# A vision transformer block with mixture of experts on one core: the shared expert moved behind the block loop, one embedding moved into the front of a stage

## The chip, the cores and the metric

The kernel runs on one core of a Trainium2 chip. The metric is the device time of one execution in microseconds. Times within the profile are microseconds from the start of the span. PE is TensorE, DVE is VectorE, ACT is ScalarE, POOL is GpSimd, SP is SyncE, which issues most DMAs.

## The reference

32 images of 36 patches and one class token give 1184 tokens of width 256, all in float32. With `ln` a normalisation without weights:

```
h = concat(cls, patches(x) @ W.T + b + pos)              # 32 x 37 x 256
# attention, per image, 16 heads of 16, no softmax
a = ln(h); q, k = silu(a Wq), silu(a Wk); v = a Wv; q, k = rope(q), rope(k)
o = ((q k^T) * lower_triangle) v * sigmoid(a Wg1 Wg2)
h = h + (ln(o) * ln_w + ln_b) @ Wo
# feed forward
y = ln(h); s = sigmoid(y @ gate.T)
# 6 of 32 experts out of the best 2 of 4 groups by s + bias; weights s / sum * 0.2
routed = sum_e w_e * (silu(y Wg_e) * (y Wu_e)) Wd_e
shared = (silu(y Sg) * (y Su)) Sd                        # hidden 128
anchor = 0.1 * the same form, one of 16 small experts
h = h + routed + shared + anchor
```

## The kernel before

The tokens lie in 11 tiles: ten of 111 tokens (three images) and one of 74. Two tiles make a block; there are six blocks, the last with one tile. `P` is 128, `D` 256, `KC` 2 (halves of the width), `BT` 222 tokens of a block, `NB` 6, `NT` 11. PSUM has eight banks, `B[0]` to `B[7]`.

**The block loop.** Each engine has its own instruction list written out by hand, and semaphores tie them. Stage j of the loop works on up to four blocks at once (`stage`): `coming` = j + 1 is embedded, `ahead` = j gets first norm, q, k, v and rope, `mid` = j - 1 gets energies, attention, gate and `Wo`, `last` = j - 2 gets second norm, routing, choice of experts, ranks in the lists and the shared expert. The order within a stage on PE is that of the loop at L612; on ACT L798, on DVE L1079. Stage 1 is the first with a `mid`, stage 2 the first with a `last`; stage 5 has no `coming`, stage 6 neither `coming` nor `ahead`.

What PE calls there, with its lines: `energies` L509 (32-row products in banks 4 to 7), `second_transposes` L552, `route` L564 (scores in bank 0), `shared_up` L590 (bank 3), `attend` L524 (bank 2), `normed_transposes` L456, `embed` L432 (12 products of 256 columns a tile, bank 0), `out_project` L538 and L541 (bank 3 for the first tile of a block, 7 for the second), `rank` L576 to L581 (bank 1), `project` L466 and L472, `rotate` L487, `gate_inner` L479, `shared_down` L601 (bank 0), `gate` L495. Each float32 product of PE leaves two records in the trace.

On DVE: `mask_energy` L1014 (four masks a tile), `shared_mult` L1051, `apply_gate` L1024, `choose` L912 to L952, `attended` L1035 to L1043, `place` L961 to L968 (gives `slot_ok`), `embedded` L976, `rope` L997 to L1007, `norms` L896 to L899, `shared_add` L1057. On ACT: `second_norm` and `first_norm` L731, `second_copy` L783, `shared_silu` L794, `scores` L789 (Sigmoid), `normed_copy` L743, `squares` L774, `qkv_copies` L749 (Silu) to L757, `split_heads` L768, `gate_tanh` L762.

**Bank 0 and its order.** `embed`, `route` and `shared_down` share bank 0. So `embed` of block b waits for the sigmoids of block b - 3 (`rt_ok`), `route` for `shared_add` of the block before (`hs_ok`) and for `h_emb`, and `shared_down` for `h_emb` too.

**The lists.** When `place` has given a block's slots, GpSimd scatters each tile's rows to the lists in DRAM, seven scatters a tile (L388): first the anchor row of both tiles, then the six expert rows of each. Three scatters of tile 9 stand behind the anchor row of tile 10. So the 14 scatters of a full block and, from block 4 on, the last 21 are in one queue, and behind them on the same engine are the additions of the list stage (L408).

**Behind the loop** the last block is routed and ranked, DVE computes a table of list tiles (L1114 to L1151), PE turns it into a row (`table_rows`, L608 and L610). SP then waits for the anchor scatters and for the table and loads rows (L355). The list stage takes 112 tiles of 128 rows: transposes (L673), up (L685), down (L694), weighing on ACT (L851), addition to `sums_d` on GpSimd (L408). PE begins it behind `hs_ok` = `NB`, the last shared addition. The weights of all experts replace the buffers of the block loop in `W`: `load_late` is issued by SP when `h_emb` and `h2_ok` say that those buffers are free.

The functions are printed with the line numbers of the profile:

Of the kernel before, what the change touches and what calls it, by code (L numbers as in the profile page):

```python
# [24 lines left out]
P = 128  # L25
D = 256
# [50 lines left out]
def build(nc, pt, wt, posr, brow, wqkv, wo, wg1, wg2, lnwb, gwt, gbias, sgu, sd, wx,  # L77
          ident_c, cmask_c, turn_c, parity_c, cs_c, before_c, small_c, out):
    with ExitStack() as ctx:
# [70 lines left out]
        g1T = sb("g1T", [HD, BT])  # L150
        s_gate = sb("s_gate", [P, BT])
        s_hid = sb("s_hid", [P, BT])
        e_sb = sb("e_sb", [P, 2 * HEADS * TT])
# [264 lines left out]
        def _(pe):  # L418
            def embed(b, i):
                t, at = BLOCKS[b][i], i * TT  # L420
                if b:
                    pe.wait_ge(ld[f"patch{b}"], 16)
                if i == 0 and b:
                    pe.wait_ge(h_emb, b)
                    if b == 2:
                        pe.wait_ge(fold_ok, 1)
                    if b >= 3:
                        pe.wait_ge(rt_ok, b - 2)
                for c in range(PC):
                    if b == 0 and i == 0:  # L430
                        pe.wait_ge(chunk[c], 32)
                    m = pe.matmul(B[0][0:TILES[t], i * D:(i + 1) * D], patch_view(b)[:, c, at:at + TILES[t]],  # L432
                                  w_patch[:, c, :], start=c == 0, stop=c == PC - 1)
                if i == len(BLOCKS[b]) - 1:
                    m.then_inc(emb_ps, 1)
# [93 lines left out]
            def out_project(b):  # L529
                pe.wait_ge(og_ok, b + 1)  # L530
                if b == 0:
                    pe.wait_ge(fold_ok, 1)
                else:
                    pe.wait_ge(sh_ok, b)
                for t in BLOCKS[b]:
# [18 lines left out]

            def route(b):
                pe.wait_ge(x2T_ok, b + 1)
                if b:
                    pe.wait_ge(hs_ok, b)
                if b + 2 < NB:
                    pe.wait_ge(h_emb, b + 3)  # L560
                for t in BLOCKS[b]:
                    (i, _), n, r = within(b, t), TILES[t], t * TT
                    for k in range(KC):
                        m = pe.matmul(B[0][0:n, i * EXPERTS:(i + 1) * EXPERTS], x2T[:, k, r:r + n], w_route[:, k, :],  # L564
                                      start=k == 0, stop=k == KC - 1)
                m.then_inc(rt_ps, 1)
# [18 lines left out]
            def shared_up(b):  # L585
                n, r = SIZES[b], FIRST[b]
                pe.wait_ge(h2_ok, BLOCKS[b][-1] + 1)
                for m in range(2):
                    for k in range(KC):
                        mm = pe.matmul(B[3][:, m * BT:m * BT + n], w_sgu[:, k, m * P:(m + 1) * P], x2T[:, k, r:r + n],  # L590
                                       start=k == 0, stop=k == KC - 1)
                mm.then_inc(su_ps, 1)

            def shared_down(b):
                pe.wait_ge(sh_ok, b + 1)
                pe.wait_ge(rt_ok, b + 1)
                if b + 3 < NB:
                    pe.wait_ge(h_emb, b + 4)
                for t in BLOCKS[b]:
                    (i, at), n = within(b, t), TILES[t]  # L600
                    m = pe.matmul(B[0][0:n, i * D:(i + 1) * D], s_hid[:, at:at + n], w_sd[:, :], start=True, stop=True)  # L601
                m.then_inc(sd_ps, 1)
# [9 lines left out]
            for j in range(-1, NB + 1):  # L612
                coming, ahead, mid, last = stage(j)
                tiles = BLOCKS[mid] if mid is not None else []
                if mid is not None:
                    energies(mid, tiles[0])
                if last is not None:
                    second_transposes(last)
                for t in tiles[1:]:
                    energies(mid, t)  # L620
                if last is not None:
                    route(last)
                    shared_up(last)
                if mid is not None:
                    attend(mid, tiles[0])
                if ahead == 0:
                    pe.wait_ge(ld["consts"], 16 * 8)
                if ahead is not None:
                    normed_transposes(ahead)
                for t in tiles[1:]:  # L630
                    attend(mid, t)
                if ahead == 0:
# [3 lines left out]
                    gate(ahead)  # L636
                if coming is not None:
                    embed(coming, 0)
                if mid is not None:
                    out_project(mid)  # L640
                if last is not None:
                    rank(last)
                if coming is not None and len(BLOCKS[coming]) > 1:
                    embed(coming, 1)
                if ahead == 0:
                    pe.wait_ge(ld["rest"], 16 * 8)
                    fold()
                elif ahead is not None:
                    project(ahead)
                    rotate(ahead)  # L650
                    gate_inner(ahead)
                if last is not None:
                    shared_down(last)
                if ahead is not None and ahead > 0:
                    gate(ahead)
            second_transposes(NB - 1)
            route(NB - 1)
            shared_up(NB - 1)
            rank(NB - 1)
            table_rows()  # L660
            shared_down(NB - 1)
# [48 lines left out]
        def _(act):  # L710
# [74 lines left out]
            def scores(b):  # L785
                act.wait_ge(rt_ps, b + 1)
                for t in BLOCKS[b]:
                    i, n = t - BLOCKS[b][0], TILES[t]
                    m = act.activation(sig[0:n, i, :], B[0][0:n, i * EXPERTS:(i + 1) * EXPERTS], ACT.Sigmoid)  # L789
                m.then_inc(rt_ok, 1)  # L790

            def shared_silu(b):
                act.wait_ge(su_ps, b + 1)
                act.activation(s_gate[:, 0:SIZES[b]], B[3][:, 0:SIZES[b]], ACT.Silu).then_inc(ss_ok, 1)  # L794

            act.wait_ge(ini, 1)
            act.activation(warm[:, :], ones[:, 0:1], ACT.Silu)
            for j in range(0, NB + 1):  # L798
# [6 lines left out]
                if last is not None:  # L805
                    shared_silu(last)
                    scores(last)
# [13 lines left out]
            scores(NB - 1)  # L821
            shared_silu(NB - 1)

# [39 lines left out]
        def _(dve):  # L863
# [184 lines left out]
            def shared_mult(b):  # L1048
                n = SIZES[b]
                dve.wait_ge(ss_ok, b + 1)  # L1050
                dve.tensor_tensor(s_hid[:, 0:n], s_gate[:, 0:n], B[3][:, BT:BT + n], ALU.mult).then_inc(sh_ok, 1)  # L1051

            def shared_add(b):
                dve.wait_ge(sd_ps, b + 1)
                t0, k, n = BLOCKS[b][0], len(BLOCKS[b]), TILES[BLOCKS[b][0]]
                rows = h[0:n, t0:t0 + k, :]
                dve.tensor_tensor(rows, B[0][0:n, 0:k * D].rearrange("p (k d) -> p k d", k=k), rows, ALU.add).then_inc(hs_ok, 1)  # L1057

# [20 lines left out]
            for j in range(-1, NB + 1):  # L1079
                coming, ahead, mid, last = stage(j)  # L1080
                for t in BLOCKS[mid] if mid is not None else []:
                    mask_energy(mid, t)
                if last is not None:
                    shared_mult(last)
                if mid is not None:
# [17 lines left out]
                if ahead == 0:  # L1103
                    dve.wait_ge(ld["rest"], 16 * 8)
                    fold()
                    add_bias(ahead)
                if last is not None:
                    shared_add(last)
            choose(NB - 1)
# [12 lines left out]
            step(dve.tensor_tensor(starts, ends, tiles_of, ALU.subtract))  # L1122
            shared_mult(NB - 1)

# [21 lines left out]
            dve.tensor_scalar(weight_c, weight_c, float(D), None, ALU.add).then_inc(cols_ok, 1)  # L1146

            dve.wait_ge(table_ps, 1)
            dve.tensor_copy(table[:, :, :].rearrange("p a b -> p (a b)"), B[6][0:1, 0:3 * P])

            dve.tensor_scalar(fresh[:, :], B[6][:, 3 * P:4 * P], pcol, None, ALU.is_le).then_inc(table_ok, 1)  # L1151
            dve.wait_ge(table_ok, 1)
            shared_add(NB - 1)

# [117 lines left out]
```

## Time and profile before

| | |
|---|---|
| median of 3 runs | 495.29 us (494.2 to 495.57) |
| profiled execution | 495.58 us, span 493.8 us |
| block loop | 38 to 219 us |
| end of the loop, table, first list rows | 219 to 247 us |
| list stage | 246 to 471 us |
| last sums and output | 471 to 494 us |

Read it in that order: each part has a different limit, and the engines' shares over the whole span say little. The granted clock is given as a share of full speed: 1.00 is 2.4 GHz, 0.50 is 1.2 GHz, and a value between is a mean over a stretch with both.

### The profile page before, as it was taken

The numbers are of one execution on the slowest core, as the hardware profiler recorded it, in microseconds if no ns is written. First come the engines' busy times: TensorE is split into PE (matmuls) and PEld (weight loads), VectorE is DVE, ScalarE is ACT, GpSimd is POOL, SyncE is SP. The second block draws the span as 40 slices with busy tenths as digits, with TensorE's granted clock in tenths as the row PEclk, the third lists the DMA queues.
The fourth block names the chain that finished last, engine by engine and source line by source line (L and its number), as shares of the span: only waits on it lengthen the run. The fifth ranks groups of instructions, "written<-read, shape, count | busy, mean of one in ns | idle before, by whom it ended". The sixth has DMA issues, their size and how long they took to land.

```text
span 493.8 us, 10106 instructions
## 1 busy us (share of the span) xinstructions
PE 370.2 (75%) x2456; PEld 302.3 (61%) x2457; DVE 261.3 (53%) x1088; ACT 203.1 (41%) x581; POOL 291.4 (59%) x205
## 2 busy tenths in 40 slices
PE   6488989989899786641277879999998898998000
PEld 4465858768677565531156557778887787787000
DVE  0336585957948848378145554444444444444045
ACT  1131143232332332210035556767776767767100
POOL 3000000383682863878587888888888888888533
PEclk9797978969879668655669999999999999999655
DMA  8999996032133861378458999999999999997795
GB/s 242 306 336 306 439 365 212 18 78 63 39 86 82 344 140 20 82 236 293 103 140 153 161 155 155 157 151 155 158 152 155 157 150 155 158 153 120 143 255 177
DMA packets 66303, 85.81 MB, mean 174 GB/s; under 512 B 16840, under 2 KB 61302, under 8 KB 65894
## 3 DMA queue, kind: packets, MB, share of 16 engines
q1 hardware_dynamic: 35734, 59.82, 39.1%
q0 software_dynamic: 29680, 24.95, 34.9%
q10 hardware_dynamic: 864, 0.73, 0.5%
q8 instruction: 12, 0.20, 0.2%
q14 instruction: 13, 0.11, 0.1%
HBM read 45.86 MB, written 39.47 MB: 173 GB/s over the span
## 4 chain that ended last, share of the span: by engine, by line
DVE 20%; PE 19%; issue 19%; DMA 17%; ACT 10%; POOL 8%; ACTq 4%; SPq 1%; DVEq 0%; POOLq 0%
DMA sums_d<-e_sb,tok 13%; POOL rows_d L388 5%; ACT UPW L831 4%; PE B L524 3%; PE B L590 3%; ACTq L274 3%; PE B L509 3%; PE B L432 2%; POOL sums_d L408 2%; ACT e_sb L851 2%; DMA W<-in_brow 2%; DMA W<-sums_d 2%; PE B L564 2%; PE B L466 2%; DVE h L1186 1%
## 5 line engine op out<-in xcount | busy, mean ns | idle before, releaser
L408 POOL DMA_INDIRECT sums_d<-e_sb,tok x112 | 174.0, 1554 | 35.3 <-issue 23.5
L388 POOL DMA_INDIRECT rows_d<-xrow,slot x77 | 105.2, 1366 | 146.0 <-issue 114.7
L685 PEld LDWEIGHTS B<-e_sb,UPW 128*128 128x128 f32 x796 | 105.7, 193 | 10.7 <-issue 5.2
L685 PE MATMUL B<-e_sb,UPW 128*128 128x128 f32 x796 | 109.7, 279 | 0.0
L694 PE MATMUL B<-W,e_sb 128*128 x224 | 73.5, 410 | 20.3 <-DVE e_sb L1177 10.3
L1177 DVE TENSOR_TENSOR e_sb<-e_sb,B 128x128 f32<-128x128 f32 (+1 forms) x112 | 32.2, 288 | 81.1 <-ACT e_sb L839 61.1
L831 ACT COPY UPW<-W 128x512 f32 (+1 forms) x112 | 63.0, 563 | 17.9 <-issue 17.7
L673 PE MATMUL B<-ident,e_sb 128*128 128x128 f32 x224 | 44.8, 283 | 14.1 <-DMA e_sb<-rows_d 13.1
L694 PEld LDWEIGHTS B<-W,e_sb 128*128 128x128 f32 x224 | 34.0, 191 | 33.5 <-issue 33.0
L851 ACT ACTIVATE e_sb<-B,wcol 128x256 f32<-128x256 f32 x112 | 53.0, 473 | 0.2 <-issue 0.2
L1161 DVE COPY e_sb<-B 128x256 f32<-128x256 f32 x112 | 46.9, 419 | 11.2 <-PE B L673 10.4
L850 ACT COPY tok<-tok_of 128x1 int32 (+1 forms) x112 | 21.5, 192 | 58.4 <-DMA sums_d<-e_sb,tok 44.8
L673 PEld LDWEIGHTS B<-ident,e_sb 128*128 128x128 f32 x224 | 28.0, 145 | 17.6 <-issue 10.7
L839 ACT ACTIVATE e_sb<-B 128x128 f32<-128x128 f32 (+1 forms) x112 | 30.7, 275 | 19.6 <-PE B L685 11.9
L432 PE MATMUL B<-W 128*111 128x256 f32 (+1 forms) x132 | 34.3, 414 | 4.7 <-DMA W<-in_pt 4.7
L432 PEld LDWEIGHTS B<-W 128*111 128x111 f32 (+1 forms) x132 | 24.0, 189 | 12.1 <-DMA W<-in_pt 5.1
L1163 DVE TENSOR_TENSOR wcol<-e_sb,fresh (+1 forms) x112 | 17.8, 159 | 24.9 <-issue 21.7
L509 PE MATMUL B<-W 32*111 32x222 f32 (+1 forms) x176 | 21.3, 521 | 11.5 <-ACT W L768 9.1
L1014 DVE TENSOR_TENSOR e_sb<-B,causal 111x444 f32<-111x444 f32 (+1 forms) x44 | 23.5, 596 | 6.4 <-PE B L509 6.3
L749 ACT ACTIVATE W<-B 128x444 f32<-128x444 f32 (+1 forms) x12 | 6.0, 500 | 44.3 <-PE B L466 44.3
L509 PEld LDWEIGHTS B<-W 32*111 32x111 f32 (+1 forms) x176 | 13.6, 239 | 16.3 <-ACT W L768 10.6
L1186 DVE TENSOR_TENSOR h<-h,W 112x256 f32<-112x256 f32 (+3 forms) x15 | 12.7, 867 | 19.0 <-DMA W<-sums_d 11.4
(165 smaller groups left out, 470.7 us busy)
## 6 DMA issues: line engine op xcount, KB each, us to landing
e_sb<-rows_d SPq DMA_DIRECT2D x112, 152.5 KB
rows_d<-padrow SPq DMA_DIRECT2D x1, 7320.0 KB, 34.5
W<-in_wx SPq DMA_DIRECT2D x1, 7027.0 KB, 50.4
sums_d<-padrow SPq DMA_DIRECT2D x4, 1408.0 KB, 22.4
W<-in_wx SPq DMA_DIRECT2D x1, 4781.0 KB, 17.2
W<-in_wx SPq DMA_DIRECT2D x1, 4576.0 KB
W<-in_pt SPq DMA_DIRECT2D x4, 666.0 KB, 8.8
sums_d<-e_sb,tok POOLq DMA_INDIRECT x112
```

The lines of the kernel that those rows point to most:

```text
L388: pool.indirect_dma_start(rows_d, bass.IndirectOffsetOnAxis(ap=slot[0:n, t, j:j + 1], axis=0), xrow[0:n, t, :], None).then_inc(done, 16)
L408: pool.indirect_dma_start(sums_d[c], bass.IndirectOffsetOnAxis(ap=tok[:, c:c + 1], axis=0), Y[:, c, :], None, compute_op=ALU.add).then_inc ...
L432: m = pe.matmul(B[0][0:TILES[t], i * D:(i + 1) * D], patch_view(b)[:, c, at:at + TILES[t]], w_patch[:, c, :], start=c == 0, stop=c == PC - 1)
L509: m = pe.matmul(B[4 + r][0:n, 2 * k * n:2 * (k + 1) * n], qk[strip, KC + k, at:at + n], q_two[strip, :, k, at:at + n], start=True, stop=True)
L673: m = pe.transpose(B[u % 2][:, k * P:(k + 1) * P], G[:, u % 4, k * P:(k + 1) * P], ident[:, :])
L685: mm = pe.matmul(B[2 + u % 2][:, m * P:(m + 1) * P], UPW[:, u % 2, at:at + P], GT[:, u % 2, k, :], start=k == 0, stop=k == KC - 1)
L694: pe.matmul(B[6 + u % 2][:, 0:D], H[:, u % 2, :], W[:, bass.ds(e, size)][:, at:at + D], start=True, stop=True).then_inc(D_ps, 1)
L831: act.copy(UPW[:, u % 2, 0:n], weights[:, 0:n]).then_inc(upw_ok, 1)
L839: act.activation(S[0:n, u % 2, :], B[2 + u % 2][0:n, 0:P], ACT.Silu).then_inc(silu_ok, 1)
L851: act.activation(Y[:, u % 4, :], B[6 + u % 2][:, 0:D], ACT.Copy, scale=wcol[:, bass.ds(i, 1)]).then_inc(Y_ok, 1)
L1161: dve.tensor_copy(GT[:, v % 2, :, :].rearrange("p k s -> p (k s)"), B[v % 2][:, 0:D]).then_inc(gt_ok, 1)
L1177: dve.tensor_tensor(H[0:n, u % 2, :], S[0:n, u % 2, :], ups, ALU.mult).then_inc(H_ok, 1)
```

## The change

`route` writes its scores to bank 3 in place of bank 0, so the waits of `embed`, `route` and `shared_down` on each other fall away, and `out_project` waits for the sigmoids (`rt_ok`). `shared_up`, `shared_silu`, `shared_mult`, `shared_down` and `shared_add` leave the loop on all three engines. They run for all six blocks behind it, `shared_up` in banks 4 and 5 in turn, `shared_down` in banks 0 and 3, with two buffers each of `s_gate` and `s_hid`. On PE block 0's `shared_up` stands ahead of the last `rank`; on DVE two multiplications and one addition stand in and behind the table's computation, the others behind it, ahead of the first list rows.

In a stage, the first tile's embedding moves from ahead of `out_project` to right behind the first tile's energies (in stages 1 to 4; stage 0 keeps it behind the gate). The first attend moves ahead of `route`, `normed_transposes` behind the last attend, and the second tile's embedding ahead of `rank`.

```diff
 # embed
-                    if b >= 3:
-                        pe.wait_ge(rt_ok, b - 2)
 # out_project
-                    pe.wait_ge(sh_ok, b)
+                    pe.wait_ge(rt_ok, b)
 # route: B[0] -> B[3]
-                if b:
-                    pe.wait_ge(hs_ok, b)
-                if b + 2 < NB:
-                    pe.wait_ge(h_emb, b + 3)
+                pe.wait_ge(h2_ok, BLOCKS[b][-1] + 1)
 # shared_up: B[3] -> B[4 + b % 2]
-                pe.wait_ge(h2_ok, BLOCKS[b][-1] + 1)
+                if b < 2:
+                    pe.wait_ge(en_ok, 4 * NT)
+                else:
+                    pe.wait_ge(sh_ok, b - 1)
 # shared_down: B[0] -> B[3 * (b % 2)]
-                pe.wait_ge(rt_ok, b + 1)
-                if b + 3 < NB:
-                    pe.wait_ge(h_emb, b + 4)
+                if b < 2:
+                    pe.wait_ge(rt_ok, NB)
+                else:
+                    pe.wait_ge(hs_ok, b - 1)
 # the stages on PE
                     energies(mid, tiles[0])
+                if coming is not None and ahead != 0:
+                    embed(coming, 0)
                 if last is not None:
                     second_transposes(last)
                 for t in tiles[1:]:
                     energies(mid, t)
+                if mid is not None:
+                    attend(mid, tiles[0])
                 if last is not None:
                     route(last)
-                    shared_up(last)
-                if mid is not None:
-                    attend(mid, tiles[0])
+                for t in tiles[1:]:
+                    attend(mid, t)
                 if ahead == 0:
                     pe.wait_ge(ld["consts"], 16 * 8)
                 if ahead is not None:
                     normed_transposes(ahead)
-                for t in tiles[1:]:
-                    attend(mid, t)
                 if ahead == 0:
                     project(ahead)
                     rotate(ahead)
                     gate_inner(ahead)
                     gate(ahead)
-                if coming is not None:
                     embed(coming, 0)
                 if mid is not None:
                     out_project(mid)
+                if coming is not None and len(BLOCKS[coming]) > 1:
+                    embed(coming, 1)
                 if last is not None:
                     rank(last)
-                if coming is not None and len(BLOCKS[coming]) > 1:
-                    embed(coming, 1)
...
-                if last is not None:
-                    shared_down(last)
-                if ahead is not None and ahead > 0:
                     gate(ahead)
 # PE behind the loop
             route(NB - 1)
-            shared_up(NB - 1)
+            shared_up(0)
             rank(NB - 1)
-            table_rows()
+            for b in range(1, NB):
+                shared_up(b)
+                if b == 2:
+                    table_rows()
+                shared_down(b - 1)
             shared_down(NB - 1)
 # ACT: out of the loop, behind the last scores
-                    shared_silu(last)
-            shared_silu(NB - 1)
+            for b in range(NB):
+                shared_silu(b)
 # DVE: out of the loop, in and behind the table
-                if last is not None:
-                    shared_mult(last)
-                if last is not None:
-                    shared_add(last)
-            shared_mult(NB - 1)
+            shared_mult(0)
...
+            shared_mult(1)
+            shared_add(0)
             dve.wait_ge(table_ps, 1)
...
             dve.wait_ge(table_ok, 1)
+            for b in range(2, NB):
+                shared_mult(b)
+                shared_add(b - 1)
             shared_add(NB - 1)
```

## Rows read from the trace of the kernel before

**Rows 1.** Windows from first energies to gate, stages 2 to 6, one gate to energies
```profile
core 0: us, PE busy (x) PEld busy (x) DVE busy (x) ACT busy (x) POOL busy (x), PEclk, DMA share, GB/s
67.38:80.26 12.88, 11.93 (x121) 9.16 (x122) 5.67 (x15) 5.32 (x11) 0.00 (x0) 0.60 1.07 378
...
99.57:113.54 13.97, 12.64 (x121) 9.85 (x122) 6.28 (x16) 5.43 (x11) 11.24 (x9) 0.63 0.33 76
113.54:132.79 19.25, 18.10 (x95) 14.76 (x95) 17.46 (x80) 5.32 (x12) 8.60 (x6) 1.00 0.20 45
132.79:146.49 13.70, 13.27 (x124) 10.22 (x125) 6.28 (x17) 5.32 (x11) 11.10 (x9) 0.63 0.35 82
...
165.11:179.57 14.46, 12.91 (x118) 9.84 (x118) 6.42 (x16) 4.70 (x10) 11.72 (x10) 0.58 0.90 274
...
194.41:205.51 11.10, 8.19 (x68) 6.45 (x68) 3.84 (x15) 3.55 (x8) 9.20 (x7) 0.54 0.32 68
```

**Rows 2.** Timeline of POOL: start, us, engine, line, operation, [idle before <-releaser]
```profile
192.40 1.48 POOL L388 DMA_INDIRECT rows_d<-xrow,slot  x1 [10.45 <-DVE slot L968]
...
217.50 1.35 POOL L388 DMA_INDIRECT rows_d<-xrow,slot  x1 [2.10 <-DVE slot L968]
...
256.20 1.62 POOL L408 DMA_INDIRECT sums_d<-e_sb,tok  x1 [0.30 <-issue]
```

**Rows 3.** Timeline of ACT, stage 3 and the first result of the lists
```profile
114.79 1.28 ACT L749 ACT_TABLE_LOAD   x1
124.12 0.54 ACT L749 ACTIVATE W<-B 128x444 f32<-128x444 f32 x1 [8.05 <-PE B L466]
...
254.07 0.47 ACT L851 ACTIVATE e_sb<-B,wcol 128x256 f32<-128x256 f32 x1
```

**Rows 4.** Timeline of PE, stage 1
```profile
38.83 1.02 PE L509 MATMUL B<-W 32*111 32x222 f32 x16
42.23 2.95 PE L509 MATMUL B<-W 32*111 32x222 f32 x16 [2.37 <-DVE e_sb L1014]
...
49.32 3.63 PE L432 MATMUL B<-W 128*111 128x256 f32 x12
...
55.24 2.83 PE L432 MATMUL B<-W 128*111 128x256 f32 x12
```

**Rows 5.** Timeline of DVE, stages 1 and 3
```profile
40.18 0.77 DVE L1063 SCALAR_TENSOR_TENSOR W<-B,W 128x256 f32<-128x256 f32 x2
...
44.49 2.20 DVE L1014 TENSOR_TENSOR e_sb<-B,causal 111x444 f32<-111x444 f32 x4 [0.84 <-PE B L509]
...
129.22 1.14 DVE L1005 TENSOR_TENSOR W<-B,cossin 128x444 f32<-128x444 f32 x2
```

**Rows 6.** Timeline of PE, stage 3
```profile
101.91 0.84 PE L552 MATMUL B<-ident,xrow 111*128 111x111 f32 x4 [1.33 <-ACT xrow L731]
102.68 2.62 PE L509 MATMUL B<-W 32*111 32x222 f32 x16
105.24 1.70 PE L564 MATMUL B<-w_route,x2T 128*111 128x32 f32 x8
...
112.50 0.98 PE L524 MATMUL B<-e_sb,W 111*32 111x111 f32 x32
113.41 2.85 PE L432 MATMUL B<-W 128*111 128x256 f32 x12
...
129.60 1.12 PE L601 MATMUL B<-w_sd,s_hid 128*111 128x256 f32 x4
```

**Rows 7.** Timeline of PE: `shared_up` in stage 3
```profile
106.75 3.31 PE L590 MATMUL B<-x2T,w_sgu 128*128 128x222 f32 x8
```

**Rows 8.** Window of stage 3 at the lower clock (columns as in rows 1)
```profile
102.40:112.40 10.00, 10.00 (x70) 7.84 (x69) 3.62 (x7) 3.44 (x7) 8.17 (x7) 0.50 0.35 82
```

**Rows 9.** Timeline of PE: first energies of stage 5, last `shared_up`, first list rows
```profile
165.11 1.83 PE L509 MATMUL B<-W 32*111 32x222 f32 x16 [3.05 <-ACT W L768]
...
221.26 1.97 PE L590 MATMUL B<-x2T,w_sgu 128*128 128x74 f32 x8
...
246.79 0.66 PE L673 MATMUL B<-ident,e_sb 128*128 128x128 f32 x2 [8.31 <-DMA e_sb<-rows_d]
```

More of the change, by code:

```diff
@@ L150, in build @@
         g1T = sb("g1T", [HD, BT])
-        s_gate = sb("s_gate", [P, BT])
-        s_hid = sb("s_hid", [P, BT])
+        s_gate = sb("s_gate", [P, 2, BT])
+        s_hid = sb("s_hid", [P, 2, BT])
         e_sb = sb("e_sb", [P, 2 * HEADS * TT])
@@ L563, in route @@
                     for k in range(KC):
-                        m = pe.matmul(B[0][0:n, i * EXPERTS:(i + 1) * EXPERTS], x2T[:, k, r:r + n], w_route[:, k, :],
+                        m = pe.matmul(B[3][0:n, i * EXPERTS:(i + 1) * EXPERTS], x2T[:, k, r:r + n], w_route[:, k, :],
                                       start=k == 0, stop=k == KC - 1)
@@ L585, in shared_up @@
             def shared_up(b):
-                n, r = SIZES[b], FIRST[b]
-                pe.wait_ge(h2_ok, BLOCKS[b][-1] + 1)
+                n, r, bank = SIZES[b], FIRST[b], B[4 + b % 2]
+                if b < 2:
+                    pe.wait_ge(en_ok, 4 * NT)
+                else:
+                    pe.wait_ge(sh_ok, b - 1)
                 for m in range(2):
                     for k in range(KC):
-                        mm = pe.matmul(B[3][:, m * BT:m * BT + n], w_sgu[:, k, m * P:(m + 1) * P], x2T[:, k, r:r + n],
+                        mm = pe.matmul(bank[:, m * BT:m * BT + n], w_sgu[:, k, m * P:(m + 1) * P], x2T[:, k, r:r + n],
                                        start=k == 0, stop=k == KC - 1)
@@ L595, in shared_down @@
                 pe.wait_ge(sh_ok, b + 1)
-                pe.wait_ge(rt_ok, b + 1)
-                if b + 3 < NB:
-                    pe.wait_ge(h_emb, b + 4)
+                if b < 2:
+                    pe.wait_ge(rt_ok, NB)
+                else:
+                    pe.wait_ge(hs_ok, b - 1)
                 for t in BLOCKS[b]:
                     (i, at), n = within(b, t), TILES[t]
-                    m = pe.matmul(B[0][0:n, i * D:(i + 1) * D], s_hid[:, at:at + n], w_sd[:, :], start=True, stop=True)
+                    m = pe.matmul(B[3 * (b % 2)][0:n, i * D:(i + 1) * D], s_hid[:, b % 2, at:at + n], w_sd[:, :],
+                                  start=True, stop=True)
                 m.then_inc(sd_ps, 1)
@@ L788, in scores @@
                     i, n = t - BLOCKS[b][0], TILES[t]
-                    m = act.activation(sig[0:n, i, :], B[0][0:n, i * EXPERTS:(i + 1) * EXPERTS], ACT.Sigmoid)
+                    m = act.activation(sig[0:n, i, :], B[3][0:n, i * EXPERTS:(i + 1) * EXPERTS], ACT.Sigmoid)
                 m.then_inc(rt_ok, 1)
@@ L793, in shared_silu @@
                 act.wait_ge(su_ps, b + 1)
-                act.activation(s_gate[:, 0:SIZES[b]], B[3][:, 0:SIZES[b]], ACT.Silu).then_inc(ss_ok, 1)
+                if b >= 2:
+                    act.wait_ge(sh_ok, b - 1)
+                act.activation(s_gate[:, b % 2, 0:SIZES[b]], B[4 + b % 2][:, 0:SIZES[b]], ACT.Silu).then_inc(ss_ok, 1)
             act.wait_ge(ini, 1)
@@ L1050, in shared_mult @@
                 dve.wait_ge(ss_ok, b + 1)
-                dve.tensor_tensor(s_hid[:, 0:n], s_gate[:, 0:n], B[3][:, BT:BT + n], ALU.mult).then_inc(sh_ok, 1)
+                if b >= 2:
+                    dve.wait_ge(sd_ps, b - 1)
+                dve.tensor_tensor(s_hid[:, b % 2, 0:n], s_gate[:, b % 2, 0:n], B[4 + b % 2][:, BT:BT + n],
+                                  ALU.mult).then_inc(sh_ok, 1)
             def shared_add(b):
@@ L1056, in shared_add @@
                 rows = h[0:n, t0:t0 + k, :]
-                dve.tensor_tensor(rows, B[0][0:n, 0:k * D].rearrange("p (k d) -> p k d", k=k), rows, ALU.add).then_inc(hs_ok, 1)
+                dve.tensor_tensor(rows, B[3 * (b % 2)][0:n, 0:k * D].rearrange("p (k d) -> p k d", k=k), rows, ALU.add).then_inc(hs_ok, 1)
             def fold():
```

## The prediction

> **What bounds the kernel now.** I began with the page's slices, where TensorE's granted clock falls again and again in the block loop and stays high in the list stage. The profiled execution took 495.58 us, its span 493.8; the median of the runs is 495.29, so the sum below is made against 495.58 and brought down by 0.3 at its end.
>
> Then the windows of the block loop [rows 1], cut at two events of each stage: the first energies on PE and `apply_gate` on DVE. From the first energies to the gate (the front) a stage takes 12.88, 13.97, 13.70, 14.46 and 11.10 us; from the gate to the next first energies (the back) 19.25 in a full stage. In the back DVE is busy 17.5 us of 19.3: choice, norms, placing and rope in one chain. In the front DVE is busy about 6 us and waits for PE. So in a front PE's order sets the time, in a back DVE's. The clock is 0.54 to 0.63 of full in a front and 1.00 in a back: the chip grants 1.2 GHz over most of the front.
>
> Next GpSimd [rows 2]. A scatter takes 1.35 us and 0.30 before the next: 1.65. The 14 of one block begin at 192.40; the first of the next block at 217.50, after an idle time of 2.10. From there 21 scatters run (21 × 1.65 = 34.7; a gap of 4 us is in the rest), and the first addition of the list stage follows directly at 256.20. The first result of the list stage is ready at 254.07 + 0.47 = 254.54 [rows 3], so GpSimd binds here, by 1.7 us. The change touches nothing of the 112 list tiles. What the change gives is therefore how much earlier the scatters of blocks 8, 9 and 10 end.
>
> **Stage 1 (38 to 67).** Between the first tile's energies, over at 39.85, and the second tile's, which begin at 42.23 because the masks are late, PE has nothing [rows 4]. After the change the first tile's embedding stands there. It waits for `fold_ok`, given at 40.95 [rows 5], so it runs from 41.0 to 43.8 (2.85 us, the embedding at the full clock [rows 6]). The second energies follow to about 45, DVE's four masks, 2.20 us as before [rows 5] and begun with the first of these energies, end at 46.7, and the last attend takes 0.98 [rows 6]: gate at 47.7 against 49.46. The old front is followed by a 3.63 us embedding and `out_project` to 55.24 [rows 4]; now `out_project` (2.3) has ahead of it only the wait for the gate, some 0.7 us, and in it that for the squares, 0.6. The second tile's embedding would begin near 51.5 instead of 55.24. Gain 3.7 us, 2.5 if the clock falls here as it did before.
>
> **Fronts of stages 2, 3, 4.** Removed: `shared_up`, 3.31 us [rows 7], and `normed_transposes` (four small products, about 0.6) moves behind the last attend. Added: embedding of one tile, between the first energies and the second transposes. A wait of 1.33 us for the second norm, which stood there [rows 6], is covered. The price of the embedding depends on the clock: 2.85 at the full clock, at the half clock up to nearly twice that, 5.4; no row shows it wholly at half (3.63 is mixed [rows 4]). In stage 3 the clock was at 0.50 from 102.4 to 112.4 [rows 8], after a pause on PE, and 1.00 before and behind. The pause before the first energies now gets longer, because PE loses 4.0 us of work in the back (2.85 embedding, 1.12 `shared_down` [rows 6]) and gains some 1.5 of waiting. So I take it that the clock falls, and that twelve dense 256-column records bring it back before the front ends: 4.3 us, between the ends. The front is then: first energies 1.83 [rows 9], embedding 4.3, transposes 0.9, second energies 1.8 (1.02 [rows 4] to 2.62 [rows 6]), attend 0.98, route 1.0 (1.70 at the half clock; at full between half of that and 1.70), attend 0.98 = 11.8 us. Gains 1.1, 2.2 and 1.9: 5.2 together. Wholly at the full clock the front is 1.02 + 2.85 + 0.6 + 1.02 + 0.98 + 1.70 + 0.98 = 9.1: gains 3.8, 4.9, 4.6 = 13.3. Wholly at half it is 1.83 + 5.4 + 1.0 + 2.62 + 1.7 + 1.7 + 1.7 = 15.9: a loss of 3.0, 1.9 and 2.2 = 7.1.
>
> **The backs stay.** PE after the gate: wait for gate and squares, `out_project` to +3.6, embedding of the second tile +6.3, `rank` +7.6 (its `ch_ok` comes at +5), `project` 3.1, values 1.8, `rotate` 1.6: +14.1. DVE needs the rotated halves at +15.7 (129.22 against the gate at 113.54 [rows 1, 5]), so there are 1.6 us of cover; it was 0.4 before. If the clock is still half through `out_project` and this embedding (+1.5 and +2.7), the cover is gone and rope is late by some 2.6 us in that stage. `shared_mult` (0.4) and `shared_add` (0.68) leave DVE: the first stood in its wait, the second delays masks that nobody waits for; nothing. Removing the `rt_ok` wait and moving the scores to Wo's bank make `out_project` wait for the sigmoids; these follow `route` by 0.4 us while the last attend takes 0.98, so nothing.
>
> The sigmoid needs its own table in each stage, and the Silu of q and k the other; these two loads of 1.28 us stay. ScalarE does the load ahead of the wait for the operand [rows 3]: its load is at 114.79, the Silu at 124.12 after 8.05 us of waiting. So both lie in its idle time. Were the sigmoid's load behind `route` all the same, load and sigmoids would take 1.28 + 0.3 = 1.6, against 0.98 + 0.62 for attend and gate that choice waits for anyway: nothing either way. The Trainium skill ("ScalarE: Activation LUTs", What ACT_TABLE_LOAD costs) gives 2.66 us for a switch with its drain and would have the calls batched by set. By its figure, with the load behind `route`, choice would come 1.4 us late in each of stages 2 to 5, and the sum would be 5.4 us less; the trace has the load ahead of the wait.
>
> **Stage 5 (165 to 194)** has no embedding to take in. Front: 1.83, wait 0.55, transposes 1.0, energies 2.6, attend 1.7, route 1.7, attend 1.7 = 11.1, and of the old front's 14.46 us PE is busy 12.91 [rows 1], so that beside the wait of 0.55 another 1.0 is idle that I can't explain and leave in for a third: 11.4 against 14.46, gain 3.1 (2.4 to 3.4).
>
> **Stage 6 (194 to 217).** `shared_up` (3.3) is gone, the table load no longer follows a late Silu (1.28): choice starts 7.1 us after the first energies, not 11.4 (the front of 11.10 and the gate's 0.3): 4.3 earlier. But GpSimd has the block before to scatter, from 192.40 to 215.40, and it started again at 217.50 [rows 2]. Of its 2.10 idle us it can lose all but the usual 0.30: it gains 1.8 only.
>
> **The shared tail.** All of it moves behind the loop: five blocks of 3.3 up and 2.0 down at the half clock plus the small one. It must be done before PE takes the first list rows (246.79 [rows 9]; those wait for a load that waits for the anchor scatters), and 1.7 us of slack follow. In times of the old trace and at the half clock: up(0) 221.3 [rows 9] to 224.8, `rank` to 226.3, up(1) to 229.6, down(0) to 231.8, up(2) to 235.1, table rows at 235.8 as now. Then down(1), up(3), down(2), up(4), down(3), up(5), down(4), down(5): 3 × 2.0 + 2 × 3.3 + 2.0 + 2.0 + 1.0, some 17 at half, 9 at the full clock, from 238 or 239: `hs_ok` at 248 to 256. All of this comes 4.3 − 1.8 = 2.5 earlier against GpSimd: 245.5 to 253.5 against 246.8 + 1.7. Dense work has then gone on from 221, so I take the fast end: nothing. The slow end costs 5.0.
>
> **Sum.** 3.7 + 5.2 + 3.1 + 1.8 = 13.8. 495.58 − 13.8 = 481.8 by the profile, 481.5 as a median.
>
> **The rivals.**
> *Clock stays up* (0.15): the dense embedding prevents the fall. For it: in stage 1 PE pauses 1.2 us, not 2.4. Against: the pause will be about 3 us, as the one before 165.11 [rows 9], and that front had 0.58 in the mean [rows 1]. 13.3 instead of 5.2: 473.4.
> *Clock stays down through the fronts* (0.14): −7.1 instead of 5.2, stage 1 at 2.5: 495.0; halfway, 489. For it: ten microseconds at 0.5 in the old front of stage 3 [rows 8] with energies and dense products mixed.
> *The tail is exposed* (0.12): half clock through it: 481.5 + 5.0 = 486.5.
> *TensorE becomes the chain in stages 2 to 4* (0.04, the slower one): half clock reaches into the back; the front loses 2.4 in the mean and rope is 2.6 late, 5.0 a stage. Stages 1, 5, 6 give 8.6, so it decides from 3.4 us lost a stage on (1.5 us over no change); at 5.0 it is 495.3 − 8.6 + 15.0 = 501.7.
> *The change does nothing* (0.03): the list stage's start hangs on something that doesn't move, weights in W say; but `load_late` is itself released by `h_emb` and `h2_ok`, which move: 495.
>
> The main case has the rest, 0.52, with 478 to 485 of its own. What a measurement here can't tell from no change is 0.3%, 1.5 us. Faster takes main, warm, tail and four fifths of the cold one; same the do-nothing case and a part of the cold one: 0.91, 0.05, 0.04. The range reaches from the warm case to the middle of the cold one: 473.5 to 490.
>
> **What would show it.** The first scatter after 210 some 14 us earlier (near 204) and 14 scatters before it without a gap; fronts of 11 to 12 us in stages 2 to 4, stage 5 near 11.4; `out_project` in stage 1 ending near 51.5; embeddings after the first energies at 3.6 to 5.0 us; backs still 19.3; the last `shared_add` before or just at the first landing of list rows. Wrong it would be if the embedding takes over 5 us and the clock is 0.5 up to the gate, if DVE waits for `rotate` in a back, or if PE's first list transposes follow the last shared product at once, later than 8 us ahead of GpSimd's first addition.

## The result and the profile after

The changed kernel takes 478.28 us (median of 4 runs) against 494.75 before: a ratio of 0.9673, interval 0.9632 to 0.9713, so 16.5 us less. Its span is 476.3 us against 493.8. Forecast were 481.5, with 473.5 to 490 as the range. Each ratio in this text is to the kernel before as it ran on the same occasion, with a 95% interval; its medians there lie between 494.2 and 497.0 us, so versions of different occasions are compared by their ratios.

The windows of the block loop in the changed kernel, cut as in [rows 1]: first energies to gate (front), gate to first energies (back), stages 2 to 6. Line numbers of the changed kernel are 2 lower on PE in the loop and 6 higher on DVE.

```profile
core 0: us, PE busy (x) PEld busy (x) DVE busy (x) ACT busy (x) POOL busy (x), PEclk, DMA share, GB/s
...
64.17:72.62 8.45, 7.98 (x121) 6.28 (x122) 5.27 (x14) 4.56 (x9) 0.00 (x0) 1.00 1.02 365
72.62:91.93 19.31, 14.99 (x82) 12.28 (x82) 17.52 (x80) 5.74 (x13) 5.14 (x4) 0.95 0.51 171
91.93:102.72 10.79, 10.31 (x121) 7.73 (x122) 5.40 (x15) 4.55 (x9) 8.66 (x8) 0.77 0.32 71
...
121.97:133.06 11.09, 10.62 (x121) 7.31 (x122) 5.45 (x15) 4.55 (x9) 8.96 (x8) 0.75 0.34 81
133.06:151.92 18.86, 15.66 (x70) 13.00 (x70) 16.94 (x78) 5.74 (x13) 10.43 (x8) 0.82 0.51 168
151.92:160.40 8.48, 7.20 (x110) 5.63 (x110) 5.28 (x15) 4.06 (x8) 6.76 (x6) 0.80 0.88 321
160.40:176.22 15.82, 13.26 (x65) 11.63 (x64) 13.41 (x72) 4.09 (x10) 9.43 (x7) 0.65 0.45 100
176.22:181.17 4.95, 3.56 (x55) 2.63 (x55) 2.80 (x13) 2.55 (x5) 4.03 (x4) 0.50 0.30 74
```

The fronts of stages 2 to 5 went from 12.88, 13.97, 13.70 and 14.46 us to 8.45, 10.79, 11.09 and 8.48, and their granted clock from about 0.6 to 0.75 and more. The backs of stages 2 and 3 stayed at 19.3.

PE in the front of stage 3 (timeline, as [rows 6]). The pause of 3.69 us before it is new (it was 1.20); the first energies and most of the embedding run at the half clock, and all behind them at the full one.

```profile
91.93 1.84 PE L507 MATMUL B<-W 32*111 32x222 f32 x16 [3.69 <-ACT W L772]
93.70 4.37 PE L430 MATMUL B<-W 128*111 128x256 f32 x12
97.90 0.54 PE L550 MATMUL B<-ident,xrow 111*128 111x111 f32 x4
98.38 1.02 PE L507 MATMUL B<-W 32*111 32x222 f32 x16
99.33 0.97 PE L522 MATMUL B<-e_sb,W 111*32 111x111 f32 x32
100.23 0.96 PE L560 MATMUL B<-w_route,x2T 128*111 128x32 f32 x8
101.67 0.98 PE L522 MATMUL B<-e_sb,W 111*32 111x111 f32 x32 [0.47 <-DVE e_sb L1020]
```

GpSimd (timeline, as [rows 2]): the 14 scatters from 173.22 run into the next block's at 196.76 with no wait for slots; then one stop of 5.52 us, and the first additions.

```profile
173.22 1.48 POOL L388 DMA_INDIRECT rows_d<-xrow,slot  x1 [4.76 <-DVE slot L974]
...
196.76 1.35 POOL L388 DMA_INDIRECT rows_d<-xrow,slot  x1 [0.30 <-issue]
...
225.11 1.35 POOL L388 DMA_INDIRECT rows_d<-xrow,slot  x1 [5.52 <-issue]
...
236.68 1.62 POOL L408 DMA_INDIRECT sums_d<-e_sb,tok  x1 [0.30 <-issue]
240.75 1.59 POOL L408 DMA_INDIRECT sums_d<-e_sb,tok  x1 [2.44 <-ACT e_sb L857]
```

In the kernel before the same stop was shorter, and the second addition did not wait:

```profile
244.63 1.35 POOL L388 DMA_INDIRECT rows_d<-xrow,slot  x1 [4.28 <-issue]
...
258.12 1.59 POOL L408 DMA_INDIRECT sums_d<-e_sb,tok  x1 [0.30 <-issue]
```

So the time can be followed: at the first energies of stage 6 the gain is 194.41 − 176.22 = 18.2 us; at block 4's first scatter 217.50 − 196.76 = 20.7; at the first addition 256.20 − 236.68 = 19.5, since the stop grew by 1.2; at the end of the span 17.5. The last 2.0 went at the very start of the list stage: GpSimd waits 2.44, 0.52 and 1.04 us ahead of its second, third and fourth addition, where it waited 0.30, 0.30 and 1.46 before, and from the fourth addition (263.03 against 245.45) to the 109th the gain stays at 17.6. The chain of work now runs through transfers there (start, us, what): the last anchor row lands 9.36 us after its scatter is issued, and the load of the rows for the second result takes 5.22 us.

```profile
214.94 9.36 DMA rows_d<-xrow,slot
...
224.97 2.28 DMA e_sb<-rows_d
...
231.74 5.22 DMA e_sb<-rows_d
```

The tail: the last shared products end at about 222, and PE then waits 5.27 us for list rows.

```profile
220.62 1.49 PE L603 MATMUL B<-w_sd,s_hid 128*111 128x256 f32 x6
227.38 0.66 PE L677 MATMUL B<-ident,e_sb 128*128 128x128 f32 x2 [5.27 <-DMA e_sb<-rows_d]
```

### The profile page after: what moved, and what is told of

It is laid out like the page before. It is cut to its first block, busy times and chain, and to the rows that moved or that the text cites. A ratio compares the mean times of both kernels' runs of the same rounds, so it can differ in the third digit from the quotient of the medians.

```text
span 476.3 us, 10113 instructions
## 1 busy us (share of the span) xinstructions
PE 361.7 (76%) x2456; PEld 299.7 (63%) x2457; DVE 261.3 (55%) x1088; ACT 201.6 (42%) x581; POOL 291.6 (61%) x205
## 4 chain that ended last, share of the span: by engine, by line
DMA 29%; PE 18%; DVE 17%; issue 13%; POOL 13%; ACT 6%; ACTq 2%; SPq 1%; POOLq 0%; DVEq 0%
DMA sums_d<-e_sb,tok 22%; POOL rows_d L388 7%; POOL sums_d L408 5%; PE B L430 5%; PE B L464 3%; ACT e_sb L857 2%; PE B L507 2%; DMA rows_d<-xrow,slot 2%; DMA W<-sums_d 2%; DMA W<-in_brow 2%; DMA e_sb<-rows_d 2%; DVE e_sb L1020 2%; DVE h L1196 2%; ACTq L274 2%; PE B L522 1%
## 5 line engine op out<-in xcount | busy, mean ns | idle before, releaser
L689 PEld LDWEIGHTS B<-e_sb,UPW 128*128 128x128 f32 x796 | 108.1, 197 | 10.8 <-issue 4.5
L689 PE MATMUL B<-e_sb,UPW 128*128 128x128 f32 x796 | 111.4, 282 | 0.0
L698 PE MATMUL B<-W,e_sb 128*128 x224 | 75.1, 418 | 20.1 <-DVE e_sb L1187 18.3
L677 PE MATMUL B<-ident,e_sb 128*128 128x128 f32 x224 | 45.4, 286 | 10.2 <-DMA e_sb<-rows_d 10.0
L430 PE MATMUL B<-W 128*111 128x256 f32 (+1 forms) x132 | 35.9, 430 | 5.7 <-DMA W<-in_pt 4.5
L845 ACT ACTIVATE e_sb<-B 128x128 f32<-128x128 f32 (+1 forms) x112 | 30.8, 275 | 17.4 <-PE B L689 10.8
L464 PE MATMUL B<-W 128*128 128x222 f32 (+1 forms) x96 | 24.5, 426 | 0.6 <-ACT W L747 0.6
L464 PEld LDWEIGHTS B<-W 128*128 128x128 f32 x96 | 22.2, 255 | 1.8 <-ACT W L747 1.0
```

The source lines that it names most:

```text
L464: m = pe.matmul(B[4 + half][:, c * BT:c * BT + n], w_qkv[:, k, lo:lo + P], xnT[:, k, 0:n], start=k == 0, stop=k == KC - 1)
L677: m = pe.transpose(B[u % 2][:, k * P:(k + 1) * P], G[:, u % 4, k * P:(k + 1) * P], ident[:, :])
L689: mm = pe.matmul(B[2 + u % 2][:, m * P:(m + 1) * P], UPW[:, u % 2, at:at + P], GT[:, u % 2, k, :], start=k == 0, stop=k == KC - 1)
L698: pe.matmul(B[6 + u % 2][:, 0:D], H[:, u % 2, :], W[:, bass.ds(e, size)][:, at:at + D], start=True, stop=True).then_inc(D_ps, 1)
```

## The experiments

### The early embedding undone

The first tile's embedding stands ahead of `out_project` again, behind `normed_transposes` (cut short):

```diff
-                if coming is not None and ahead != 0:
-                    embed(coming, 0)              # behind energies(mid, tiles[0])
...
+                if coming is not None and ahead != 0:
+                    embed(coming, 0)              # ahead of out_project(mid)
```

> The changed kernel with one part undone: in stages 1 to 4 the first tile's embedding stands behind normed_transposes and ahead of out_project again. Theory (the early embedding fills PE's pauses and brings the clock up early): stage 1 loses 3.7 us again, the fronts of stages 2 to 4 are no shorter without it (about 11 us at the half clock, against 8.45, 10.79, 11.09), so 478.3 + 3.7 + 2.5 = 484.5 us. Rival (leaving the shared expert out of the front did it all, the embedding only costs there): fronts of about 8 us or less in stages 3 and 4, stage 1 alone loses: 478.3 + 3.7 - 5 = 477 us.

482.51 us, ratio 0.9782 (0.9717 to 0.9847), just clear of the changed kernel's interval. Fronts of stages 2 to 4 (windows):

```profile
66.57:76.65 10.08, 8.86 (x109) 6.94 (x110) 5.26 (x14) 4.55 (x9) 0.00 (x0) 0.63 1.07 381
96.64:107.54 10.90, 10.47 (x109) 8.04 (x110) 5.32 (x15) 4.55 (x9) 8.77 (x8) 0.50 0.34 77
127.44:138.35 10.91, 10.49 (x109) 8.05 (x110) 5.31 (x15) 4.56 (x9) 8.78 (x8) 0.50 0.33 79
```

By itself this spoke for my theory: without the embedding the fronts of stages 3 and 4 are as long, and wholly at the half clock.

### The early embedding in stage 1 alone

The edit is the same with the condition `j == 1 or j < 0` for the early place.

> The changed kernel with the early embedding in stage 1 alone; stages 2 to 4 have it ahead of out_project. Theory: stage 1 keeps its 3.7 us, stages 2 to 4 lose 2.5 to 3 in sum, most of it in stage 2, whose clock falls again: 481 us. Rival (the early embedding costs in stages 2 to 4): 474 to 476 us.

477.48 us, ratio 0.9662 (0.9611 to 0.9713): not to be told from the changed kernel. Both forecasts fell. Windows of the same fronts (the first is cut at 64.00, the energies began at 63.92):

```profile
64.00:74.00 10.00, 8.77 (x109) 6.86 (x110) 5.19 (x14) 4.48 (x9) 0.00 (x0) 0.56 0.99 353
93.32:101.64 8.32, 6.99 (x109) 5.40 (x110) 5.30 (x14) 4.55 (x9) 6.80 (x6) 0.79 0.32 74
121.42:131.59 10.17, 8.79 (x109) 6.85 (x110) 5.36 (x15) 4.55 (x9) 8.34 (x7) 0.58 0.36 81
150.32:161.13 10.81, 10.32 (x109) 7.91 (x110) 5.30 (x14) 4.06 (x8) 8.68 (x8) 0.51 0.95 302
```

Stage 2 costs 1.6 us more than in the changed kernel, stage 3 2.5 less, stage 4 0.9 less, stage 5 2.3 more. In stages 2 to 4 the move of the embedding gives nothing in sum that can be told. In stage 1 it gives 2.3 us: from its first energies to those of stage 2 this run takes 24.71 us, and 27.00 with the embedding moved back there too. And stage 3 here has the instructions of stage 3 in the run above, 109 records in both, and takes 8.32 us at a clock of 0.79 against 10.90 at 0.50. The work does not decide between these two; the clock does.

### Without the shared expert

```diff
-            shared_up(0)
             rank(NB - 1)
-            for b in range(1, NB):
-                shared_up(b)
-                if b == 2:
-                    table_rows()
-                shared_down(b - 1)
-            shared_down(NB - 1)
+            table_rows()
...
# also out: shared_silu, shared_mult, shared_add, the wait for hs_ok
```

> The changed kernel without the shared expert on any engine, so the output lacks its term. Theory (its work behind the loop is covered by the scatters and the first loads of list rows): 478 us, within 1.5. Rival (the list stage waits for it, or it disturbs the transfers): 472 to 475 us, and the first list transposes come earlier against the last scatter.

This kernel leaves the shared expert's term out of its result. 478.56 us, ratio 0.9635 (0.9551 to 0.9718). The first list transposes wait as long for their rows as with the shared expert, only from an earlier end of work:

```profile
227.48 0.66 PE L670 MATMUL B<-ident,e_sb 128*128 128x128 f32 x2 [14.30 <-DMA e_sb<-rows_d]
```

227.48 against 227.38: the tail is covered whole, and it does not slow the transfers enough to be seen. The medians alone could hide some 4 us; it is this row that shows it.

### PE kept busy in its pauses, in the changed kernel

```diff
+            def keep_busy(bank, n):
+                for _ in range(n):
+                    pe.matmul(bank[:, 0:D], ident[:, :], w_sgu[:, 0, :], start=True, stop=True)
...
+                if j in {4: 3, 5: 3}:                      # ahead of rank(last)
+                    keep_busy(B[2], {4: 3, 5: 3}[j])
...
+                if j in {2: 7, 3: 7, 4: 6}:                # behind gate(ahead)
+                    pe.wait_ge(h2_ok, BLOCKS[mid][-1] + 1)
+                    keep_busy(B[7], {2: 7, 3: 7, 4: 6}[j])
```

> The changed kernel with products that nobody reads in PE's pauses: 7, 7 and 6 of 128x256 behind gate in stages 2, 3 and 4, 3 ahead of rank in stages 4 and 5. Theory (the fronts of stages 3 and 4 are long because the pause of 3.7 us before them takes the clock to one half): first energies 1.0 instead of 1.84, embedding 2.85 instead of 4.4 and 4.7, fronts 8.5 instead of 10.8 and 11.1, no wait for rotate in stage 5: scatters 5 us earlier, 473.5 us. Rival (the pause is not the cause): fronts stay at 11, 478 us or, where the products run past the pause, 480.

472.65 us, ratio 0.9547 (0.9485 to 0.9609). Fronts of stages 2 to 5 and the back of 5:

```profile
68.10:76.55 8.45, 7.98 (x121) 6.27 (x122) 5.27 (x14) 4.56 (x9) 0.00 (x0) 1.00 1.09 385
95.87:104.32 8.45, 7.98 (x121) 6.28 (x122) 5.31 (x15) 4.56 (x9) 6.93 (x6) 1.00 0.31 74
123.91:132.34 8.43, 7.96 (x121) 5.91 (x122) 5.27 (x15) 4.55 (x9) 6.91 (x6) 1.00 0.33 78
151.16:158.43 7.27, 5.92 (x110) 4.42 (x110) 5.27 (x15) 4.05 (x8) 5.75 (x6) 1.00 1.00 386
158.43:173.27 14.84, 10.06 (x71) 8.42 (x70) 13.23 (x72) 4.16 (x11) 9.83 (x8) 0.99 0.57 125
```

All three full fronts are the same 8.4 us at 1.00, and the back of stage 5 is again the 14.84 it was before the change. With useless work added the kernel gets 5.6 us faster: in this order the pause of 3.7 us before the fronts of stages 3 and 4 was what made them long. Other profiles bear it out. The four with this order and no fillers (the changed kernel twice, the one without the shared expert, the one with nops below) all have a pause of 3.6 to 3.7 us there, first energies of 1.83 or 1.84 us, and fronts of 10.8 to 11.4. The second one with these fillers (`warm_split`, below) has pauses of 0.47 and 0.74 us, energies of 1.02 and fronts of 8.4 and 8.5.

### The same in the order before

```diff
# in the kernel before the change
+                if j in {2: 2, 3: 2, 4: 2, 5: 2}:          # behind energies(mid, tiles[0])
+                    keep_busy(B[3], 2)
...
+                if j in {2: 1, 3: 1, 4: 5}:                # behind gate(ahead)
+                    pe.wait_ge(h2_ok, BLOCKS[mid][-1] + 1)
+                    keep_busy(B[7], {2: 1, 3: 1, 4: 5}[j])
```

> The kernel before, with its own order and the shared expert in the loop, and only products that nobody reads added in PE's pauses: 2 behind the first energies of stages 2 to 5, and 1, 1 and 5 behind gate in stages 2, 3 and 4. One theory (most of what the change gave in the fronts is clock, and the old order would have had it too): shared_up takes 1.65 us instead of 3.3, fronts of stages 2 to 5 about 9.2 us against 12.9 to 14.5, 480 us. The other (the gain is the 3.3 us of work taken out of the fronts; the clock is a by-product): fronts stay over 12 us, 491 to 495 us.

483.04 us, ratio 0.9716 (0.9675 to 0.9757). Fronts of stages 2 to 6, and `shared_up` in stage 2 on the timeline:

```profile
67.27:77.16 9.89, 9.89 (x125) 7.62 (x126) 5.68 (x16) 5.33 (x11) 0.00 (x0) 0.83 1.09 383
96.46:108.61 12.15, 11.89 (x128) 8.85 (x129) 6.29 (x17) 5.32 (x11) 9.89 (x8) 0.86 0.32 75
127.90:138.21 10.31, 10.00 (x127) 7.40 (x128) 6.33 (x17) 5.32 (x11) 8.40 (x7) 1.00 0.31 74
156.79:167.13 10.34, 9.23 (x122) 6.75 (x122) 6.32 (x16) 4.58 (x10) 8.40 (x7) 1.00 1.01 325
182.04:191.43 9.39, 6.06 (x71) 4.64 (x70) 3.85 (x15) 3.68 (x8) 7.86 (x6) 0.82 0.31 65
```

```profile
73.00 1.75 PE L590 MATMUL B<-x2T,w_sgu 128*128 128x222 f32 x8
```

The same `shared_up` that took 3.31 us [rows 7] takes 1.75, in stages 4 and 5 too; in stage 3 it still takes 3.31. Fifteen small products that nobody reads (2 in each of four stages, and 7 more) give 14.0 us, nearly as much as the whole change, with the shared expert still in the loop. The fronts came out at 10 to 12 us and not at 9.2, since the clock still falls in stages 2 and 3, but the theory of the clock holds and its rival (491 to 495) falls. The change keeps a worth of its own: with fillers in both orders the ratio is 0.9716 in the old one and 0.9547 in the new one, some 8 us, in which the clock left low in stages 2 and 3 of the old one is still counted.

### Both together, and the place of the embedding again

This has the early embedding in stage 1 alone and `keep_busy` behind the first energies (2 in stages 2 to 5), ahead of `rank` (3 in stage 5) and behind `gate` (1, 3 and 5 in stages 2, 3 and 4).

> The changed kernel with the early embedding in stage 1 alone and with products that nobody reads in PE's pauses: 2 behind the first energies of stages 2 to 5, 3 ahead of rank in stage 5, 1, 3 and 5 behind gate in stages 2, 3 and 4. Theory (with the clock at full, a front is shorter without the embedding, since nothing then stands ahead of the second transposes but the wait for the second norm): fronts of stages 2 to 4 about 7.2 us against 8.45 with both, backs 19.3 to 19.8, 469.5 us against 472.65 for the fillers with all embeddings early. Rival (the early embedding is worth keeping even then, PE gets late in the backs): fronts 8.5 or backs over 20.5, 473 us or more.

466.42 us, ratio 0.9429 (0.9361 to 0.9496).

```profile
65.16:73.52 8.36, 7.88 (x113) 6.03 (x114) 5.27 (x15) 4.54 (x9) 0.00 (x0) 0.80 1.05 372
...
92.83:101.15 8.32, 7.84 (x113) 5.88 (x114) 5.41 (x15) 4.55 (x9) 6.79 (x6) 0.79 0.32 71
120.92:128.28 7.36, 6.92 (x114) 5.11 (x114) 5.35 (x14) 4.55 (x9) 5.83 (x6) 1.00 0.34 83
146.91:154.26 7.35, 6.91 (x114) 5.10 (x114) 5.35 (x14) 4.05 (x8) 5.83 (x6) 1.00 1.03 403
```

At the full clock a front without the embedding takes 7.36 us against 8.45 with it: there the early embedding costs 1.1 us a stage, since the backs, where it stands instead, take 19.31, 19.77 and 18.63 us and so grow by 0.5 in stage 3 alone. The fronts of stages 2 and 3 did not reach the 7.2 forecast; their clock was 0.80.

The same kernel on another occasion:

> The same kernel as warm_embed_stage1, for its ratio alone: 466.5 us, ratio 0.943.

469.90 us, ratio 0.9447 (0.9411 to 0.9483). No other version measured is faster beyond the noise. By the ratios it is 5.5% below the kernel before and 2.3% below the changed one. The change itself, run once more on another occasion:

> The changed kernel itself, unaltered, beside the others of this call. Both theories: 478 us, ratio 0.967; the fronts of stages 3 and 4 again 10.8 and 11.1 us, that of stage 2 again 8.45.

479.65 us, ratio 0.9682 (0.961 to 0.9753). The fronts were not all the same: stage 2 took 10.14 us at 0.83 this time.

```profile
65.50:75.64 10.14, 9.66 (x121) 7.31 (x122) 5.28 (x15) 4.56 (x9) 0.00 (x0) 0.83 1.06 376
94.95:106.27 11.32, 10.85 (x121) 8.10 (x122) 5.41 (x14) 4.54 (x9) 9.19 (x8) 0.74 0.33 74
```

### The last weight load in earlier pieces

```diff
-            sp.wait_ge(h2_ok, NT)
-            load_late(1)
+            sp.wait_ge(gate_ps, NB)
+            load_between(late[1], qkv_end)
+            sp.wait_ge(av_ps, NT)
+            load_between(qkv_end, heads_end)
+            sp.wait_ge(wo_ps, NT)
+            load_between(heads_end, late[2])
```

> The changed kernel with the last load of weights into W (4781 KB, issued when the last tile's h is ready, h2_ok) in three pieces, each issued when its part of W is free: after the last gate product, after the last attend, after the last out_project. Nothing else changes. Theory (that load fills the DMA engines while the scatters of block 4 run; they land late, GpSimd stops for 5.5 us ahead of the 15th of the last 21 scatters, and the last anchor row lands 9 us after its issue): the stop is under 2 us, list rows are loaded some 4 us earlier, 474 us. Rival (the stop belongs to that place in GpSimd's instructions, the load has nothing to do with it): the stop stays at 4 to 5.5 us at the 15th scatter, 478 us.

476.28 us, ratio 0.9613 (0.9554 to 0.9672), which overlaps the changed kernel's. The stop took 3.21 us, and between the first anchor rows of the last 21 scatters and the last one the DMA engines were at 0.38 (206 to 212 us), against 0.89 in the same window of the changed kernel:

```profile
224.82 1.35 POOL L398 DMA_INDIRECT rows_d<-xrow,slot  x1 [3.21 <-issue]
```

```profile
206.00:212.00 6.00, 4.38 (x18) 3.29 (x16) 5.28 (x26) 0.71 (x2) 4.78 (x5) 0.87 0.38 94
```

On top of the fillers it gave nothing that can be told:

> The changed kernel with the fillers of the run warm and the last weight load in three earlier pieces. Theory (two separate gains, 5.6 and 2 us): 470.5 us. Rival (the earlier pieces only move the contention): 472.7 us.

471.63 us, ratio 0.9552 (0.9498 to 0.9606), against 0.9547 without the pieces.

> warm_embed_stage1 with the last weight load in three earlier pieces. Theory (the stop of GpSimd was 2.0 us there and loading list rows waits for the anchor scatters): 464.5 us. Rival (nothing left for it to give): 466.5 us.

470.23 us, ratio 0.9446 (0.9403 to 0.9489), against 0.9447. With the pieces the stop was shorter than in the changed kernel (3.21 us against 5.52 and 5.05) and than with the fillers (3.02 against 4.57), but not in the third pair (2.39 against 2.04 and 3.65); the medians show no gain. The pieces are not worth keeping on this evidence.

### The stop of GpSimd

```diff
             pool.wait_ge(empty, 16)
+            for _ in range(24):
+                pool.nop(nofuse=True)
```

> The changed kernel with 24 instructions that do nothing ahead of GpSimd's first scatter. One theory (GpSimd's stop of 5.5 us is at a place in its instruction stream, where the next ones must be fetched): the stop moves to an earlier scatter than the 71st, 478 us or a little less. The other (a limit on scatters under way, reached when the transfers are slow): it stays ahead of the 71st, 4 to 6 us.

479.37 us in one run. The stop is ahead of the 71st scatter again:

```profile
228.43 1.35 POOL L390 DMA_INDIRECT rows_d<-xrow,slot  x1 [5.29 <-issue]
```

In all fourteen profiles, of the kernel before, the changed one and the twelve runs, the stop stands ahead of the 71st scatter, and lasts from 2.0 to 6.5 us. A place in the instruction stream should have moved with 24 more instructions. That speaks for something that counts scatters; what it is, no run tells.

## Why the prediction was right, and where its terms were off

**The chain and its places.** Front set by PE, back by DVE, the scatters behind them: right. The backs of stages 2 and 3 are 19.31 and 19.25 us, as before.

**Stage 1,** 3.7 us forecast: the first energies of stage 2 come 3.2 us earlier in a loop that began 0.62 later (39.45 against 38.83), so 3.8. Right, and the clock stayed up in it (1.00 from 39.45 to 64.17). The early embedding is 2.3 of these 3.8. The two runs with the embedding moved back and kept in stage 1 alone differ by 5.0 us in their medians; the first energies of stage 2 differ by 66.57 − 63.92 = 2.65, and the fronts of stages 3 and 4, with the same instructions at another clock, by 2.58 and 0.74.

**Fronts of stages 2 to 4,** 5.2 us forecast at 11.8 each, 10.2 measured (4.4, 3.2, 2.6). The embedding in stages 3 and 4 took 4.37 and 4.67 us, as sized (4.3). Two terms were too large: the parts behind it ran at the full clock (transposes 0.54, not 0.9; second energies 1.02, not 1.8), and stage 2 lost no clock in that execution. There the rival "clock stays up" came true; but `after_again`, with the same pause before that front (0.79 us against 0.80), lost it. (An embedding is six products and twelve records, not twelve products.)

**What stands behind that gain is a point that I had wrong.** I held that the early embedding covers a wait and brings the clock back, and that removing `shared_up` frees 3.3 us. Shown is: the clock did come back within the embedding in stages 3 and 4; but the 3.3 us were 1.75 us of work at a half clock; the early embedding gives nothing in stages 2 to 4 (0.9662 without, 0.9673 with); and filling the pauses alone gives 0.9716 in the old order. I priced the clock inside the new order and never asked what it would be worth in the old one, though [rows 1] had 0.6 in every front. The Trainium skill ("TensorE: Matmul & The Clock Gate", HAM oscillation) names pauses between bursts of products as what drops the clock. In stages 3 and 4 the runs agree: their fronts go from a clock of 0.77 and 0.75 to 1.00 with the pauses filled. But long pauses are not the whole of it: in the run with the embedding moved back the clock was 0.50 in both fronts, behind pauses of 0.80 us, and with none longer than 0.43 within them.

**Stage 5,** 3.1 forecast, 6.0 measured: the clock again, 0.80 instead of the 0.5 that I had put in. But its back went from 14.84 to 15.82, because DVE waited for `rotate` at the lower clock (0.25 and 0.54 us; 0.65 in the mean of that back), one of my signs of being wrong. I had named that mechanism for stages 2 to 4 and left it out here; with the fillers it is gone.

**Stage 6 and the scatters,** 1.8 forecast, 1.6 measured, the 14 scatters without a wait as said. But the first scatter of block 4, which I wanted near 204, came at 196.76: this sign, 7 us off, shows best that the block loop gained far more than I had priced.

**The tail,** nothing forecast: shown by the run without the shared expert. PE was done 5.27 us before its rows came, where the fast end of my sum had left 1.3.

**Given back.** I took the stop as fixed; it grew from 4.28 to 5.52. And I held that the list stage moves with the end of the scatters; it came 2.0 us less early, lost ahead of the second to fourth addition, where results of the list stage were late behind a row load of 5.22 us. `after_again` has waits of 1.75, 0.30 and 0.83 us there. That the change causes this is not shown: the early embedding in stage 1 alone has 0.30, 0.30 and 1.35, nearly as before.

**The sum.** Forecast were 13.8. The fronts of stages 2 to 4 gave 5.0 more, that of stage 5 2.9 more: 21.7. Off that go the loop's late start in this execution 0.6, the back of stage 4 0.2, stage 6 0.2, the stop 1.2 and the list stage 2.0: 17.5, the difference of the spans. Rope's lateness in the back of stage 5 is not among them, since block 3's slots are given ahead of it. The forecast was near by luck: two terms that were too small by 7.9 met losses of 4.2 that I had not counted. One slip in the range: halfway between 481.5 and 495.0 is 488.3, not 489; nothing hangs on it.

**Table loads** cost nothing that a window shows: the backs, which begin with the choice, are the 19.3 us of before. The load for the sigmoids stands ahead of the end of `route` (101.19), as said, and they begin right behind it, with no more than its own 1.28 us to be seen:

```profile
100.02 1.28 ACT L793 ACT_TABLE_LOAD   x1
101.31 0.28 ACT L793 ACTIVATE sig<-B 111x32 f32<-111x32 f32 x2
```

## What to carry to other kernels

Where a profile shows TensorE's clock at one half in the stretches that bind, first fill the pauses before them with products that nobody reads, in the order as it stands: fifteen of them gave 14 us here in one edit. Only then price a reordering, since at the half clock a product taken out looks nearly twice as dear as it is (3.31 us against 1.75). And when a part's removal shortens a stretch, compare the same instructions at both clocks before the gain is put down to the part.

## What the hardware showed that I had not expected

One and the same front, 109 records in both runs, took 8.32 us with a granted clock of 0.79 and 10.90 us with 0.50, with pauses before it of 0.86 and 0.80 us:

```profile
93.32 1.02 PE L507 MATMUL B<-W 32*111 32x222 f32 x16 [0.86 <-ACT W L774]
```

```profile
96.64 1.83 PE L507 MATMUL B<-W 32*111 32x222 f32 x16 [0.80 <-ACT W L774]
```

The first is the run with the early embedding in stage 1 alone, the second the one without it. So a front's clock is not decided by its own instructions and the pause before it alone, and two profiles of one kernel differ in it by 1.7 us (stage 2: 8.45 and 10.14). What else decides it, no run here tells. GpSimd stops once for 2.0 to 6.5 us ahead of the 71st indirect scatter in every kernel; the cause stays open.
